# Re-ordered slots in a two-layer adaLN transformer: output projection by tile, feed-forward steps and norm moved to other slots

## The reference

```python
def attn_layer(x, Wqkv, qs, ksc, Wo):            # x: (4, 512, 128)
    q, k, v = jnp.split(x @ Wqkv, 3, -1)          # 1024 each, 16 heads of 64
    q = l2norm(q) * qs ; k = l2norm(k) * ksc      # per head
    q = q * cos * scale + rotate_half(q) * sin * scale
    k = k * cos * inv + rotate_half(k) * sin * inv
    out = local_attention(q, k, v)                # softmax over the 64 keys of a window
    return out @ Wo                               # 1024 -> 128

def ffn_layer(x, g, bln, W1, b1, W2, b2):
    xn = (x - mu) / jnp.sqrt(var + 1e-05) * g + bln
    a, gate = jnp.split(xn @ W1 + b1, 2, -1)      # 341 each
    return a * jax.nn.gelu(gate, approximate=False) @ W2 + b2

for i in range(6):
    x = attn_layer(shift_tokens(x), ...) + x
    x = ffn_layer(shift_tokens(x), ...) + x
```

## Time and profile before

| | before |
|---|---|
| runs | 2194.44, 2198.6, 2200.27 us, median 2198.6 |
| profiled execution, span | 2182.5 us, 16.1 under the median of the runs (the page gives no other time of its own) |
| slots, first to last query projection | 561.3 to 2116.4 us |
| PE, PEld, DVE, ACT, POOL busy | 92, 67, 83, 72, 53% of the span |
| granted TensorE clock, mean | 0.985 of full speed |

### The profile page before, as it was taken

One profiled execution on the slowest core, in us unless ns is written; L12 is line 12 of the kernel. 1 busy time (PEld: TensorE's weight loads), 2 busy tenths in 40 slices (PEclk: granted clock), 3 DMA queues, 4 the chain that ended last, 5 costly groups with the idle time before them and its releaser, 6 DMA issues.

```text
span 2182.5 us, 82607 instructions
## 1 busy us (share of the span) xinstructions
PE 2005.7 (92%) x34395; PEld 1457.7 (67%) x34395; DVE 1809.4 (83%) x3751; ACT 1579.9 (72%) x3031; POOL 1167.3 (53%) x1413
## 2 busy tenths in 40 slices
PE   6888899987699999999999999999999999999997
PEld 4666654455577776777777777777767777677775
DVE  7888765678798998888988888988888988888884
ACT  4777753365577887787877788777787878887773
POOL 1112110000577676666776667666667767667761
PEclk9999999998899999999999999999999999999999
DMA  4000001000122232222322223322232322332221
GB/s 114 1 2 2 2 31 59 30 1 30 52 72 68 61 105 69 68 63 71 90 72 75 66 58 95 81 68 66 70 87 71 87 58 58 102 82 62 75 59 40
DMA packets 98196, 132.18 MB, mean 61 GB/s; under 512 B 27900, under 2 KB 42882, under 8 KB 97826
## 3 DMA queue, kind: packets, MB, share of 16 engines
q1 hardware_dynamic: 97826, 126.90, 22.0%
HBM read 28.20 MB, written 1.11 MB: 13 GB/s over the span
## 4 chain that ended last, share of the span: by engine, by line
PE 72%; DVE 13%; issue 6%; ACT 6%; POOL 1%; SPq 1%; DMA 0%; DVEq 0%; POOLq 0%; ACTq 0%
PE oo L586 21%; PE pj L586 19%; PE tr L589 14%; PE sc L586 13%; ACT arena L1924 3%; PE tr L586 2%; DVE arena L1729 2%; DVE xn L1318 2%; DVE arena L1486 1%; PE oo L589 1%; DVE arena L1731 1%; DVE arena L1750 1%; DVE arena L1752 1%; PE sc L589 1%; ACT sc L1924 1%
## 5 line engine op out<-in xcount | busy, mean ns | idle before, releaser
L2345 POOL TENSOR_TENSOR arena<-arena 128x1024 f32<-128x1024 f32 x192 | 456.9, 2380 | 336.9 <-DVE arena L1731 336.9
L1924 ACT ACTIVATE arena<-tr 128x512 f32<-128x512 f32 (+2 forms) x874 | 460.8, 570 | 111.9 <-PE tr L589 109.7
L1924 ACT ACTIVATE arena<-pj 128x512 f32<-128x512 f32 x576 | 341.7, 599 | 189.5 <-PE pj L586 150.4
L589 PE MATMUL tr<-ident,arena 128*128 128x128 f32 x2882 | 413.3, 279 | 25.3 <-DMA beta<-in_L_attn_betas 9.8
L1924 ACT ACTIVATE arena<-arena 128x16 f32<-128x16 f32 (+6 forms) x808 | 362.3, 454 | 98.7 <-DVE arena L1486 74.0
L589 PEld LDWEIGHTS tr<-ident,arena 128*128 128x128 f32 x2882 | 330.6, 141 | 93.4 <-issue 34.5
L2363 POOL TENSOR_TENSOR arena<-arena 128x1024 f32<-128x1024 f32 x192 | 366.7, 1910 | 23.2 <-POOL arena L2356 0.9
L1729 DVE TENSOR_TENSOR arena<-pj,rtab 128x512 f32<-128x512 f32 x384 | 259.8, 677 | 24.8 <-ACT arena L1924 23.4
L586 PE MATMUL oo<-slab,arena 64*32 64x64 f32 (+1 forms) x12416 | 232.1, 228 | 41.0 <-issue 26.4
L1731 DVE TENSOR_TENSOR arena<-pj,rtab 128x512 f32<-128x512 f32 x384 | 261.4, 681 | 0.0
L1737 DVE TENSOR_REDUCE arena<-arena 128x8 f32<-128x512 f32 x384 | 255.6, 677 | 0.0
(11 more groups left out here) (289 smaller groups left out, 3802.5 us busy)
## 6 DMA issues: line engine op xcount, KB each, us to landing
slab<-arena SPq DMA_DIRECT2D x576, 128.0 KB, 2.4
slab<-arena SPq DMA_DIRECT2D x336, 64.0 KB, 2.0
wqkv<-in_L_ffn_Wqkv SPq DMA_DIRECT2D x18, 512.0 KB, 4.2
arena<-gate_mem SPq DMA_DIRECT2D x24, 256.0 KB, 4.3
wo<-in_L_ffn_Wo SPq DMA_DIRECT2D x6, 512.0 KB, 4.2
w<-in_L_ffn_W SPq DMA_DIRECT2D x6, 341.0 KB
YT<-in_L_attn_x SPq DMA_DIRECT2D x4, 256.0 KB, 3.5
arena<-in_L_ffn_W SPq DMA_DIRECT2D x1, 1024.0 KB
```

Of the source, the lines that this page charges most:

```text
L589: return nc.tensor.transpose(o, i, ident[0:i.shape[0], 0:i.shape[0]])
L1924: return nc.scalar.activation(o, i, f, **k)
L2345: p_.tensor_tensor(r_, r_, rb[:, k, :], ALU.add).then_inc(sum_ok, 1)
```

## The change

The five functions `slot` are written in another order, and five steps are cut or placed otherwise:

- The output projection comes in quarters, one tile of 128 tokens in every slot (`wo_quarter`), always in the second bank of `oo`; quarter 0 already in slot 3 of its own sequence. The extra product goes. DVE's addition comes in quarters too.
- `ff_up` 0 and 1 stand in slot 0 and `ff_up` 2 in slot 1, all three ahead of or between the scores; `ff_down` stands in slot 3 and writes into `sc`, and its sum (`y_ff`) too comes in slot 3.
- `norm_back` comes after the first scores of slot 3, into `oo`. In slot 3 `ln_apply` stands between the rotations 0 and 1; the norm's statistics in slot 2 stand behind `soft1`. The column of biases and scales is read where it lies (`LC`), so its copy `lcur` goes.
- `project` c = 5 (second half of the values) stands last in a slot. In slots 2 and 3 `out_` stands ahead of the second scores.
- On ACT both copies of the turned probabilities (`take_probs`) come ahead of `square` 2, `inverse_root` 0 ahead of the mask, and the inverse root of the keys in the next slot, as on POOL `newton` and `scaled` of the keys. The low half of the key weights of a layer is made by POOL at the end of the slot before and not by DVE at the start of the layer.

The diff, cut: of the bodies of the slots on DVE, ACT and POOL the new order stands here, the old one stands in the listing above.

```diff
-FFB = (oo, tr, oo)
-WOB = (sc[:, 0], oo[:, 1])
+FFB = (tr, oo, oo)
 LD_W = (ld_q, ld_k, ld_v)
-LNB_BANKS = (oo[:, 0], tr[:, 0])
+LNB_BANKS = (oo[:, 0], oo[:, 0])
...
+        self.mw, self.iw = (self.n, 0) if t == 3 else (self.m1, t + 1)
+        self.lw = l if t == 3 or b >= 1 else l - 1
+        self.yw = (b if t == 3 else (b - 1) % B) * S + self.iw * P
...
         layer_end = s_.ahead is not None and b == B - 1 and t == T - 1
         if layer_end:
             qkv_weights(l + 1, 0)
+        if s_.later and b == 0 and t == 2:
+            wo_weights(l)
+        if layer_end:
+            qkv_weights(l + 1, 1)
         if s_.c_:
             windows(g - 1, (t - 1) % T)
...
-        if s_.later and b == 1 and t == 1:
+        if s_.later and b == 1 and t == 3:
             ff_weights(l)
...
         def values_(i):
+            if i == 0 and s_.mw is not None:
+                pe.wait_ge(y_att, s_.mw * T + s_.iw + 1)
             if i == 0 and t == 0 and m2 is not None:
...
+                pe.wait_ge(lnb_out, m2 + 1)
             if i == 0 and t == 1 and m2 is not None:
...
+                pe.wait_ge(ff_ev, m2 * FFC + 2)
+            if i == 0 and t == 2 and m2 is not None:
+                pe.wait_ge(ff_ev, m2 * FFC + 3)
             if i == 0 and t == 3 and m1 is not None:
                 pe.wait_ge(lnb_norm, m1 + 1)
             values(n2, g - 2, t2, i)
                 else:
                     pe.wait_ge(pt_cp, (g - 2) * 2 + j + 1)
                 if t == 0 and m2 is not None:
...
+                    pe.wait_ge(ff_ev, m2 * FFC + 1)
                 turn_out(g - 2, j)
-        def wo_half(m, i):
...
-            half = slice(i * (S // 2), (i + 1) * (S // 2))
+        def wo_quarter(m, i):
+            pe.wait_ge(o_cp, (m * T + i + 1) * 2)
+            tok = slice(i * P, (i + 1) * P)
             for p_ in range(PAIRS):
-                last = mm(WOB[i][:, half], wo[:, p_, :], oT[:, p_, half], start=(p_ == 0),
+                last = mm(oo[:, 1, tok], wo[:, p_, :], oT[:, p_, tok], start=(p_ == 0),
                           stop=(p_ == PAIRS - 1))
-            if i == 0:
-                last = mm(sc[:, 0, S // 2:S], w_hi[0][:, 0:P], xs_hi[:, 0:S // 2], start=False,
-                          skip_group_check=True)
             last.then_inc(wo_mm, 1)
         def ff_down(m):
             pe.wait_ge(ff_ev, m * FFC + 3)
+            pe.wait_ge(t_sub, g - 1)
             for k, (o, w) in enumerate(CH):
-                last = mm(oo[:, 0], w2[0:w, k, :], fa[0:w, k, :], start=(k == 0), stop=(k == FFC - 1))
+                last = mm(sc[:, 0], w2[0:w, k, :], fa[0:w, k, :], start=(k == 0), stop=(k == FFC - 1))
             last.then_inc(w2_mm, 1)
...
+        if b == 0 and t == 0:
+            pe.wait_ge(wl_ok[0], l + 1)
+        queries(0)
+        queries(1)
...
         if c_:
             turn_q()
...
+        if s_.mw is not None:
+            if b == 0 and t == 3:
+                pe.wait_ge(ld_wo, l * 16 + 16)
+            if t == 1 and m2 is not None:
+                pe.wait_ge(ff_ev, m2 * FFC + 2)
+            if t == 2 and m2 is not None:
+                pe.wait_ge(ff_ev, m2 * FFC + 3)
+            wait(pe, on_ok, g - 2)
+            wo_quarter(s_.mw, s_.iw)
+        if t == 3 and m2 is not None:
             ff_down(m2)
...
+        if b == 0 and t == 0:
+            pe.wait_ge(wl_ok[1], l + 1)
+        project(g, t, 2)
         if d_:
             probs()
...
+        project(g, t, 3)
         if d_:
             turn_k()
         if d_:
             values_(1)
...
+        if b == 0 and t == 0:
+            pe.wait_ge(wl_ok[2], l + 1)
+        project(g, t, 4)
+        if t == 0 and m2 is not None:
+            pe.wait_ge(lnb_out, m2 + 1)
+            pe.wait_ge(qk_cp, g * 4)
+            if b == 2:
+                pe.wait_ge(ld_ff, s_.l2 * 64 + 64)
+            ff_up(m2, 0, FFB[0])
         if c_:
             window_scores(g - 1, (t - 1) % T, 0)
...
+        if t < 2 and m2 is not None:
+            pe.wait_ge(on_ok, g - 1)
+            ff_up(m2, t + 1, FFB[t + 1])
         if t == 2 and m1 is not None:
             pe.wait_ge(xs_f, m1 + 1)
...
+            pe.wait_ge(on_ok, g - 1)
             norm_in(LNB, LNB_BANKS[0], xsF)
...
+        if t == 3 and m1 is not None:
+            pe.wait_ge(on_ok, g - 1)
+            norm_back(LNB, LNB_BANKS[1], m1)
+        if d_ and t >= 2:
+            out_()
         if c_:
             window_scores(g - 1, (t - 1) % T, 1)
...
+        if d_ and t < 2:
             out_()
+        project(g, t, 5)
...
+        def add_attention():
+            part = YT[:, s_.yw:s_.yw + P]
+            ve.wait_ge(wo_mm, s_.mw * T + s_.iw + 1)
+            v.tensor_tensor(part, oo[:, 1, s_.iw * P:(s_.iw + 1) * P], part, ALU.add).then_inc(y_att, 1)
+        if b == 0 and t == 0:
+            ve.wait_ge(tab_ok, l * 2 + 1)
+        wait(ve, qk_tr, (g - 2) * 4 + 2)
+        rotate(g, t, 0)
+        if t == 3 and m1 is not None:
+            ln_apply(LNB, LNB_BANKS[0], m1)
+        rotate(g, t, 1)
+        if s_.mw is not None:
+            add_attention()
+        if t == 3 and m2 is not None:
+            y = YT[:, s_.y2:s_.y2 + S]
+            ve.wait_ge(w2_mm, m2 + 1)
+            v.scalar_tensor_tensor(out=y, in0=sc[:, 0], scalar=LC(m2, 2), in1=y,
+                                   op0=ALU.add, op1=ALU.add).then_inc(y_ff, 1)
+        lengths(g, 0)
+        lengths(g, 1)
...
+        clamp(g, 0)
+        if b == 0 and t == 0:
+            ve.wait_ge(tab_ok, l * 2 + 2)
+        wait(ve, qk_tr, (g - 2) * 4 + 4)
+        rotate(g, t, 2)
+        if b == 0 and t == 0:
+            weights_low(l, 2)
+        if d_:
+            soft2(g - 2)
+        if d_:
+            weighted(g - 2)
+        rotate(g, t, 3)
+        lengths(g, 2)
+        if b == B - 1 and t == 0 and l < DEPTH - 1:
+            tables(l + 1)
+        lengths(g, 3)
+        clamp(g, 1)
         if t == 0 and m2 is not None:
             ff_gate(m2, 0, FFB[0])
...
+        if c_:
+            soft1(g - 1)
+        if t < 2 and m2 is not None:
+            ff_gate(m2, t + 1, FFB[t + 1])
         if t == 2 and m1 is not None:
             ln_stats(LNB, LNB_BANKS[0], m1, m1)
...
+        wait(ac, ss_ok, g * 4 - 1)
+        square(g, 0)
+        if g > 0:
+            inverse_root(g - 1, 1)
+        wait(ac, ss_ok, g * 4)
+        square(g, 1)
...
         if d_:
             ac.wait_ge(t_sub, g - 1)
             wait(ac, e_tr, g2 * 2)
             act(Ex, Tm, ACT.Exp, scale=8.0).then_inc(e_exp, 1)
         if c_:
             take_qk_part(g - 1, (t - 1) % T, 0)
...
             take_qk_part(g - 1, (t - 1) % T, 1)
...
+        if d_:
+            take_probs(g2, 0)
+            take_probs(g2, 1)
+        if s_.later and b == 0 and t == 0:
+            weights_high(l, 2)
+        ac.wait_ge(ss_ok, g * 4 + 1)
+        square(g, 2)
         if layer_end:
             table(g + 1, l + 1, 0)
...
+        inverse_root(g, 0)
+        if c_:
+            if t == 3 and m2 is not None:
+                ac.wait_ge(y_ff, m2 + 2)
+            mask(g - 1, (t - 1) % T)
+        ac.wait_ge(ss_ok, g * 4 + 2)
+        square(g, 3)
+        if c_:
+            take_qk_part(g - 1, (t - 1) % T, 2)
+            take_qk_part(g - 1, (t - 1) % T, 3)
         if s_.ahead is not None and t == 1:
             if l > 0 or b == B - 1:
                 ac.wait_ge(y_ff, n + 1 - B + 2)
             ac.wait_ge(pj_mm, n * (6 * T) + 6)
             shifted(xs_hi, YT[:, s_.ahead:s_.ahead + S], 0, P).then_inc(xs_h, 1)
...
+        if t == 2 and m1 is not None:
+            ac.wait_ge(y_att, m1 * T + T)
+            shifted(xsF, YT[:, s_.y1:s_.y1 + S], 0, S).then_inc(xs_f, 1)
         if layer_end:
             weights_high(l + 1, 0)
...
+        if t == 0:
             wait(ac, pj_mm, n * (6 * T))
             shifted(xs_hi, YT[:, s_.y0:s_.y0 + S], P, S).then_inc(xs_h, 1)
...
+        wait(ac, o_mm, g - T + 2)
+        copy_v(g, t, 0)
+        if t == 3 and m1 is not None:
+            ln_finish(LNB, LNB_BANKS[1], m1, LC(m1, 0), LC(m1, 1), hB)
+        if t == 0 and m2 is not None:
+            gelu(m2, 0, FFB[0])
+        if t < 2 and m2 is not None:
+            gelu(m2, t + 1, FFB[t + 1])
+            log_exp_tables()
+        if d_:
+            wait(ac, wo_mm, (g2 // T - 1) * T + t2 + 1)
+            take_out(g2, t2, 0)
+            if t >= 2:
+                take_out(g2, t2, 1)
+        copy_v(g, t, 1)
+        if d_ and t < 2:
+            take_out(g2, t2, 1)
         if layer_end:
             weights_high(l + 1, 1)
...
             table(g + 1, l + 1, 1)
...
+        if t == 3 and s_.m1 is not None:
             power(LNB, s_.m1)
...
+        if g > 0:
+            newton(g - 1, 1)
+            scaled(g - 1, (t - 1) % T, 1)
+        add_parts(g, t, 0)
+        newton(g, 0)
+        scaled(g, t, 0)
+        if t == 0:
+            low_half(n * 2 + 2, YT[:, s_.y0:s_.y0 + S], P, S)
+        if s_.ahead is not None and t == 1:
```

(9 more changed lines are left out.)

274 lines of the change are left out of this document (43 added, 231 removed).

## The result

The changed kernel took 2217.07 us (median of 4 runs, 2216.71 to 2223.2), the kernel before 2197.67 beside it (2194.44 to 2200.27): 1.0098 times as long, 95% interval 1.0084 to 1.0112, 19.4 us slower. The forecast was 2185. Timed a second time (e4) the ratio was 1.0114 (1.0089 to 1.0140).

A forecast was written before the change was run, and what follows sets the result against it. PE was taken as the bound, busy 62.70 of 65.10 us a group. Terms -27 - 3 - 7 + 5 + 8 + 7 + 6 - 3 = -14 gave 2184.6, said as 2185 us; own range 2172 to 2194, 8 in 10 range 2159 to 2215.

The forecast's parts named there:

- The waits of slot 3: PE's waits in slot 3 for DVE's rotation and `ln_apply` go: -27 us, between 0 and -29.
- The extra product: The output projection's extra product goes, 0.13 us in each of 23 cases: -3 us.
- the passage: One switch from float32 to split products goes, `ff_up` 1 to `project` 5: -7 us (0 to -7).
- Quarters: Four quarters of the output projection take longer than two halves, 7.1 against 6.9 us a group: +5 us.
- Both upper bounds: Costs of the quarters if priced by busy time per record (+38 us) or with every load paid in full (+130).
- The hand-over: At slot ends, next `project` 1 waits for ACT to copy the bank `project` 5 wrote: +8 us, bounds -8 and +57.
- The shifted copy: ACT's copy for the norm in slot 2, behind the key copies, delays `norm_in`: +7 us, bounds 0 and 29.
- The late division: Rival: slots 2 and 3, `out_` and `norm_back` wait for the division, +29 us, 2214; chance 0.19; sign over 0.3 a slot.
- DVE is the bound: Rival: PE's busy time is mostly latency, so groups shrink halfway to DVE's work: -105 us, 2094; chance 0.01.
- Layer starts: At layer starts `project` 4 waits for the value weights' low half on DVE, behind `square` 2: +6 us.
- Ends: Last sequence's early quarter and last turn of queries save time: -3 us; bounds -6 and +4, for first slots too.
- The waits without a cause: PE's idle times unexplained by the profile, 26.4 us ahead of the values: no change; growth over 10 us means wrong.

The follow-up runs named there:

- e4: The changed kernel, unchanged, timed and profiled again: 2226.82 us, ratio 1.0114 to the kernel before.
- e5: The changed kernel with `project` 5 put back ahead of the transposes of the outputs and the second scores: 2252.18 us, ratio 1.0243 to the kernel before.
- e9: e1 with ScalarE doing `square` 2 ahead of the value weights' conversion in a layer's first slot: 2201.7 us, ratio 1.0021 to the kernel before.
- e1: The changed kernel with the next layer's rotation tables moved to the end of the same slot, behind gate 1: 2206.09 us, ratio 1.0024 to the kernel before.
- e12: The changed kernel with GpSimd's second addition waiting for the tables in the first slot of a layer's last block: 2206.07 us, ratio 1.0027 to the kernel before.
- e6: The changed kernel with the load of the output projection weights issued behind the windows of values again: 2214.5 us, ratio 1.0060 to the kernel before.
- e3: The changed kernel with GpSimd's power for a normalization in the first slots moved forward: 2223.96 us, ratio 1.0101 to the kernel before.
- e13: The changed kernel with e1, e3, e6, e9's edits, key weights' load behind the windows, most weight loads in pieces: 2180.73 us, ratio 0.9919 to the kernel before.

## Why the prediction was wrong

Its sum comes out right for the ordinary slot, in part by luck, and leaves the layer boundaries out. Step by step, by its own names:

- **The waits of slot 3 (-27)**: right. 28.4 us before, and nothing of it in the steady slots after.
- **The extra product (-3) and the passage (-7)**: right. The product is gone. Behind `ff_up` 1 the first product of `project` 5 took 0.64 us; in its new place it takes 0.32, and only the passage behind `ff_down` is left at 0.63.
- **Quarters (+5)**: a quarter lasts 1.71 us to the next key projection, 1.79 ahead of `ff_down`, a half 3.45. Four make 6.9 and two 6.9: +0.0. Both upper bounds (38, 130) were far off; the distance of starts was the right row to take.
- **The hand-over (+8)**: 7.6, the mechanism too (e5's rows).
- **The shifted copy (+7)**: never the last thing waited for. In most groups it has ended 0.34 us before `norm_in` starts, and what `norm_in` waits for is the division.
- **The late division** (a rival): its mechanism is there at a third of its size, 11.9 us of waits in 35 slots in place of 29. They do not stand where it put them: 15 ahead of `ff_up` 1 in slot 1, 14 ahead of `norm_in` in slot 2, 6 ahead of `norm_back` in slot 3 (0.34 us at most, just over its sign of being wrong), all but none ahead of `out_`. I gave it as all or nothing. The sum got its -17 for the ordinary slots (without starts and ends) with 12 us for quarters and copy that did not come and without these 12 that did: two misses that cancel.
- **DVE is the bound** (a rival): no. In slot 0 TensorE is busy 17.10 of 17.10 us, VectorE 14.44.
- **Layer starts (+6)**: the step that failed. It counted the one instruction that I had seen move, the low half of the value weights. `project` 4 does wait for it (1.4 us, e9's row), and slot 0 of a first block loses half of what was forecast (1.3 us beyond an ordinary one, 0.7 before: 3 us). It has no term for `tables`, which in the diff stands unchanged two lines below `crossing(g, 3)`. The instructions around it had moved: gate 0 from far ahead of it to behind it, the release of GpSimd's addition from well before it to right before it. e1 and e12 price that at 16 us: 2.2 us a layer in which VectorE and GpSimd shut each other out, 0.6 for the place, and the lower clock behind the stand. Nor has it one for SyncE's order of loads: e6 puts the output weights at 8 to 12 us by its time (1.0060 against 1.0098 and 1.0114), 2 to 5 by the five slots of single profiles.
- **Ends (-3)**: -2.9 in the last three slots and -2.4 behind them (-1.0 in e4), but +5.7 in the first group, where 2.3 to 3.5 were GpSimd's powers (e3's trace). "For the first slots too" was said of a bound of +4 and worked out from nothing.
- **The waits without a cause**, set at no change: all rows "issue" together make 53.1 us, 46.8 before, under the 10 us of growth given as a sign of being wrong (against the first profile, with 37.7, they are over it). They hold two things. In slot 0 of a last block "issue" was a gate that VectorE owed (13.8 us, e1 takes it away). The others stand where a block of 256 instructions begins, and did not grow.

Sum: 20 groups x -0.76 = -15; +32 at the boundaries, +7 for the first group and its start, -5 at the end, -0.3 in the two groups left over: +18, as the spans differ. Of the 32 at the boundaries 16 are shown (the tables). e13 shows what was there to win: 2180.7, below the forecast of 2185, with the same order of the ordinary slot.

Left open: the other 16 us of the boundaries, which no experiment takes apart by kind; why TensorE's next instructions come late at some blocks and not at others, and why executions of one kernel differ so; and what pieces gain and what the place of the loads does.

## What to carry over

Price a reordering at the rare slots too: list what runs once per layer (tables, conversions, loads), and for each ask what it is now ahead of, even where its own line in the diff has not moved. Where VectorE has an operation on two operands in on-chip memory, look what GpSimd does at that moment; a wait that keeps the two apart can be worth more than it costs. Stands without a named cause can be counted through the engine's list: here all but those ahead of `out_` fell on one place of 256. And take a second profile of the base before explaining a difference of under 1%.

## What was unexpected of the hardware

- A VectorE multiplication of 0.49 us (two of 128x128) lasted 2.65 beside a GpSimd addition of 2.65, and a subtraction of 1.22 lasted 1.99; rotations that read the accumulators did not slow down. In these two of five layers the addition grew too, from 2.36 to 2.65; in the other three it kept its 2.35, and the multiplication before, 0.41 alone, lasted 2.6.
- A stand of TensorE of 2.75 us was followed by products at the 1.2 GHz level (starts 0.43 apart, elsewhere 0.23) in seven of ten cases (the changed kernel and e4), and not in the other three, with the same stand at the same place; behind stands of 0.59 and 0.95 us the products came at 0.23 at once.
- TensorE's stands "for issue" break a group at the same product in different executions (61 of 64, 44 of 64, 51 of 64), because they fall on every 256th entry of its list, and the instruction queue brings one packet for each 256. Most such places cost nothing, 40 of 248 cost 0.3 to 3.2 us.
- Executions of one kernel on one chip lay up to 19 us apart (e4), and a single profile can be 15 us off the median.
